# Mixing on four 32-row tiles of the array in place of a block-diagonal matrix

## The reference

```python
x: (32, 32, 256)   itok: (32,) in 1..198   weights: (200, 32, 32)
w_gate, w_up: (256, 1024)   w_down: (1024, 256)          # all float32

w = weights[itok]                                # a 32x32 matrix for each of 32 samples
y = einsum('bct,bcd->bdt', x, w)                 # the mixing
h = silu(y @ w_gate) * (y @ w_up)                # (32, 32, 1024)
h = of every 4 neighbours the 2 largest by magnitude, the others 0
out = x + h @ w_down
```

## Time and profile before

| | |
|---|---|
| median of three runs | 83.60 us |
| the profiled execution, its own time | 83.66 us |
| its span, first to last instruction | 81.7 us |
| PE busy | 75.5 us (92%) |
| DVE busy | 61.2 us (75%) |
| ACT busy | 42.9 us (53%) |
| mean granted TensorE clock | 0.994 |

### The profile page before, as it was taken

One profiled execution on the slowest core, in us unless ns is written; L12 is line 12 of the kernel. 1 busy time (PEld: TensorE's weight loads), 2 busy tenths in 40 slices (PEclk: granted clock), 3 DMA queues, 4 the chain that ended last, 5 costly groups with the idle time before them and its releaser, 6 DMA issues.

```text
span 81.7 us, 983 instructions
## 1 busy us (share of the span) xinstructions
PE 75.5 (92%) x338; PEld 59.8 (73%) x338; DVE 61.2 (75%) x93; ACT 42.9 (53%) x65; POOL 8.0 (10%) x13
## 2 busy tenths in 40 slices
PE   3996699999999999999999999999999999999920
PEld 1331688898888888888888888888888888888800
DVE  0003799178389999996899999999999999991060
ACT  6000983595863986975392699995770006410000
POOL 7500000000000070013000000442000000000000
PEclk9999999999999999999999999999999999999997
DMA  0792899977400049915800000399950000006024
GB/s 0 138 326 113 251 325 335 429 237 285 201 0 0 0 88 199 195 32 96 160 4 0 8 4 0 64 193 201 205 108 0 0 0 0 0 0 257 0 92 164
DMA packets 3076, 9.62 MB, mean 118 GB/s; under 512 B 480, under 2 KB 480, under 8 KB 2816
## 3 DMA queue, kind: packets, MB, share of 16 engines
q1 hardware_dynamic: 2160, 6.29, 22.3%
q0 software_dynamic: 912, 3.28, 20.9%
HBM read 5.37 MB, written 1.05 MB: 79 GB/s over the span
## 4 chain that ended last, share of the span: by engine, by line
PE 84%; DMA 8%; DVE 3%; ACT 1%; issue 1%; DVEq 0%
PE bank L536 50%; PE y_banks L573 13%; PE bank L573 13%; DMA h<-in_table,rows_sb 5%; PE y_banks L521 5%; PE bank L547 4%; DMA cond_sb<-in_cond 2%; DVE gate_raw L428 2%; ACT h L237 1%; DVE h L347 1%; DVE rows_sb L432 0%; DVEq L427 0%
## 5 line engine op out<-in xcount | busy, mean ns | idle before, releaser
L536 PE MATMUL bank<-y_hl,up_hl 128*128 128x512 f32 x96 | 24.2, 389 | 0.0
L536 PE MATMUL bank<-y_hl,gate_hl 128*128 128x512 f32 x84 | 21.4, 390 | 0.0
L536 PEld LDWEIGHTS bank<-y_hl,up_hl 128*128 128x128 f32 x96 | 18.0, 188 | 3.8
L536 PEld LDWEIGHTS bank<-y_hl,gate_hl 128*128 128x128 f32 x84 | 15.7, 188 | 3.2
L243 ACT ACTIVATE silu<-bank 128x512 f32<-128x512 f32 x16 | 9.4, 595 | 8.5 <-PE bank L536 8.2
L264 ACT ACTIVATE h_hl<-h 128x1024 fp32r<-128x1024 f32 (+1 forms) x8 | 6.7, 844 | 8.5 <-DVE h L414 8.4
L573 PE MATMUL y_banks<-h_hl,down_hl 128*128 128x512 f32 x48 | 11.0, 389 | 0.0
L573 PE MATMUL bank<-h_hl,down_hl 128*128 128x512 f32 x48 | 11.0, 389 | 0.0
L573 PEld LDWEIGHTS y_banks<-h_hl,down_hl 128*128 128x128 f32 x48 | 9.0, 188 | 1.9
L573 PEld LDWEIGHTS bank<-h_hl,down_hl 128*128 128x128 f32 x48 | 9.0, 188 | 1.9
L378 DVE TENSOR_TENSOR h<-bank,silu 128x512 f32<-128x512 f32 x12 | 8.1, 684 | 1.9 <-ACT silu L243 1.9
(11 more groups left out here) (40 smaller groups left out, 71.9 us busy)
## 6 DMA issues: line engine op xcount, KB each, us to landing
h_hl<-h POOLq DMA_DIRECT2D x4, 512.0 KB, 5.2
up_raw<-in_w_up SPq DMA_DIRECT2D x2, 512.0 KB, 5.8
down_raw<-in_w_down SPq DMA_DIRECT2D x1, 1024.0 KB, 9.5
gate_raw<-in_x_t SPq DMA_DIRECT2D x1, 1024.0 KB, 5.0
down_hl<-down_raw POOLq DMA_DIRECT2D x2, 512.0 KB, 5.5
out<-gate_raw SPq DMA_DIRECT2D x4, 256.0 KB, 2.3
x_sb<-in_x SPq DMA_DIRECT2D x2, 256.0 KB, 4.0
gate_raw<-in_w_gate SPq DMA_DIRECT2D x2, 256.0 KB, 4.4
```

Source lines behind the costliest of these rows:

```text
L536: last = nc.tensor.matmul(dst, w_hl[w][:, s, q, k, j], y_hl[:, m, half, k], start=i == 0, stop=i == len(terms) - 1)
```

## The change

The block-diagonal matrix is gone: POOL no longer zeroes it and ACT and DVE no longer copy blocks. Each 32x32 matrix is used where the transpose leaves it, by a matmul of 32 rows (one sample's channels), 128 stationary columns (a block k of x) and 32 moving columns. The four samples of a group use the array's rows 0 to 31, 32 to 63, 64 to 95 and 96 to 127, and write to four different PSUM banks. `mixing(half)` thus has 32 products where it had 8, and raises `mixed` once, at its end, where it raised it after each k. y of half 0 lies in banks 0 to 3, y of half 1 in banks 2 to 5; the pairs sit in banks 4-5, 6-7 and 0-1. `mixing(1)` is moved behind pair 2 and also waits for `product(0)`, since banks 4 and 5 held pair 0. The DVE's y_lo of half 0 waits for both pieces of y_hi, and `first_gates` takes the two y_lo terms last. Samples are dealt to halves and groups in another order on the host.

```diff
-        ring = [ctx.enter_context(nc.psum_tensor(f"bank{i}", [P, TH], f32)) for i in range(2 * RING)]
-        y_banks = ctx.enter_context(nc.psum_tensor("y_banks", [P, KT, TH], f32))
+        banks = ctx.enter_context(nc.psum_tensor("banks", [P, 8, TH], f32))
+        Y_BANK = 2
+        y_banks = banks[:, Y_BANK:Y_BANK + KT]
+        PLACES = [4, 6, 0]
+        MIX_BANKS = [0, Y_BANK]
+        MIX_PAIR = 3
+        def place(n):
+            return n % RING if n < MIX_PAIR else (n - MIX_PAIR + 1) % RING
+        def mixed_y(half, k, end):
+            y = banks[:, MIX_BANKS[half]:MIX_BANKS[half] + NB, 0:KT * P]
+            return y.rearrange("p r (k n) -> p k r n", k=KT)[:, k:end]
+        def split_y(part, half, k, end):
+            return y_hl[:, part, half, k:end].rearrange("p k (r n) -> p k r n", r=NB)
...
-            nc.gpsimd.memset(mix_diag, 0.0).then_inc(zero_done, 1)
...
             def high_y(half, k, end):
-                act.wait_ge(mixed, KT * half + end)
-                nc.scalar.activation(y_hl[:, HI, half, k:end], y_banks[:, k:end], ACT.Copy).then_inc(y_hi, 1)
+                act.wait_ge(mixed, half + 1)
+                nc.scalar.activation(split_y(HI, half, k, end), mixed_y(half, k, end), ACT.Copy).then_inc(y_hi, 1)
...
-            diagonal(ACT_FIRST)
...
-            diagonal(ACT_LAST)
...
             def low_y(i):
                 half, k, end = Y_PIECES[i]
-                dve.wait_ge(mixed, KT * half + end)
-                dve.wait_ge(y_hi, i + 1)
+                dve.wait_ge(y_hi, KT if half == 0 else i + 1)
...
-            diagonal(DVE_FIRST)
...
-            diagonal(DVE_LAST)
...
             def mixing(half):
+                pe.wait_ge(transposed, 1)
                 pe.wait_ge(x_in[half], 32 if half == 0 else 16)
                 if half > 0:
                     pe.wait_ge(y_lo, KT * half)
+                    pe.wait_ge(h_done, 1)
                 for k in range(KT):
                     for i in range(GH):
                         g = half * GH + i
...
-                        last = nc.tensor.matmul(y_banks[:, k, i * P:(i + 1) * P],
-                                                x_sb[:, g, k * P:(k + 1) * P],
-                                                mix_diag[:, g].rearrange("p b d -> p (b d)"),
-                                                start=True, stop=True)
-                    last.then_inc(mixed, 1)
+                        for r in range(NB):
+                            rows = slice(r * C, (r + 1) * C)
+                            last = nc.tensor.matmul(mixed_y(half, k, k + 1)[:, 0, r, i * D:(i + 1) * D],
+                                                    x_sb[rows, g, k * P:(k + 1) * P],
+                                                    mix_w[rows, g * D:(g + 1) * D],
+                                                    start=True, stop=True)
+                last.then_inc(mixed, 1)
...
-                terms = [(s, m, k) for k in range(KT) for s, m in ((HI, HI), (LO, HI), (HI, LO))]
+                terms = [(s, HI, k) for k in range(KT) for s in (HI, LO)] + [(HI, LO, k) for k in range(KT)]
...
             def gate_up(n):
-                if n >= RING:
-                    pe.wait_ge(h_done, n - RING + 1)
+                if n == MIX_PAIR + RING - 1:
+                    pe.wait_ge(y_lo, len(Y_PIECES))
+                elif n >= MIX_PAIR:
+                    pe.wait_ge(h_done, n - RING + (2 if n < MIX_PAIR + RING - 1 else 1))
...
-                if n == 2:
+                if n == MIX_PAIR:
                     mixing(1)
```

More of the change, by code:

```diff
@@ L74, in adaln_ffn @@
         mix_w = h[:, 1, 1, 0:NG * D]
-        mix_diag = h[:, 1, 2:4].rearrange("p m t -> p (m t)").rearrange(
-            "p (g b d) -> p g b d", g=NG, b=NB)
         far = sb("far", [P, 4, TH], bf16)
@@ L92, in adaln_ffn @@
         rows_done = sem("rows_done")
-        zero_done = sem("zero_done")
         transposed = sem("transposed")
-        diag_done = sem("diag_done")
-        diag_act_done = sem("diag_act_done")
         mixed = sem("mixed")
@@ L122, in adaln_ffn @@
         block = ctx.enter_context(nc.Block())
+        def place(n):
+            return n % RING if n < MIX_PAIR else (n - MIX_PAIR + 1) % RING
         def gate_bank(n):
-            return ring[2 * (n % RING)]
+            return banks[:, PLACES[place(n)]]
         def up_bank(n):
-            return ring[2 * (n % RING) + 1]
+            return banks[:, PLACES[place(n)] + 1]
+        def mixed_y(half, k, end):
[3 more added lines that the diff above has]
+            return y_hl[:, part, half, k:end].rearrange("p k (r n) -> p k r n", r=NB)
         def down_bank(half, k):
-            return y_banks[:, k] if half == 0 else (gate_bank(ACC_PAIR), up_bank(ACC_PAIR))[k][:]
+            return y_banks[:, k] if half == 0 else (gate_bank(ACC_PAIR), up_bank(ACC_PAIR))[k]
         Y_PIECES = [(0, k, k + 1) for k in range(KT)] + [(1, 0, KT)]
[L136 to L149, removed]
         PIECES = [(0, w, k, k + 1) for w in range(2) for k in range(KT)] + \
@@ L242, in gate_silu @@
                     act.wait_ge(h_done, n - 2)
-                nc.scalar.activation(silu[:, n % 3], gate_bank(n)[:], ACT.Silu).then_inc(silu_done, 1)
+                nc.scalar.activation(silu[:, n % 3], gate_bank(n), ACT.Silu).then_inc(silu_done, 1)
             def absolute(n):
@@ L348, in transpose_rows @@
                                     mix_row.rearrange("p (e c) -> p e c", e=D8)).then_inc(transposed, 1)
[L350 to L354, removed]
             def low_weights(i):
@@ L364, in low_y @@
                 half, k, end = Y_PIECES[i]
-                dve.wait_ge(mixed, KT * half + end)
-                dve.wait_ge(y_hi, i + 1)
-                nc.vector.tensor_tensor(y_hl[:, LO, half, k:end], y_banks[:, k:end],
-                                        y_hl[:, HI, half, k:end].bitcast(f32), ALU.subtract).then_inc(y_lo, 1)
+                dve.wait_ge(y_hi, KT if half == 0 else i + 1)
+                nc.vector.tensor_tensor(split_y(LO, half, k, end), mixed_y(half, k, end),
+                                        split_y(HI, half, k, end).bitcast(f32), ALU.subtract).then_inc(y_lo, 1)
             def product(n):
@@ L377, in product @@
                     dve.wait_ge(h_lo_sent[0][j // 2], 16)
-                nc.vector.tensor_tensor(hs[u][:, j], up_bank(n)[:], silu[:, n % 3],
+                nc.vector.tensor_tensor(hs[u][:, j], up_bank(n), silu[:, n % 3],
                                         ALU.mult).then_inc(h_done, 1)
@@ L507, in warm_up @@
                 for _ in range(times):
-                    nc.tensor.matmul(ring[0][:], warm[:, 0:P], warm[:], start=True, stop=True)
+                    nc.tensor.matmul(gate_bank(0), warm[:, 0:P], warm[:], start=True, stop=True)
             def mixing(half):
+                pe.wait_ge(transposed, 1)
                 pe.wait_ge(x_in[half], 32 if half == 0 else 16)
@@ L546, in first_gates @@
                     for n in (0, 1):
-                        nc.tensor.matmul(gate_bank(n)[:], w_hl[0][:, s, 0, k, n], y_hl[:, m, 0, k],
+                        nc.tensor.matmul(gate_bank(n), w_hl[0][:, s, 0, k, n], y_hl[:, m, 0, k],
                                          start=i == 0, stop=i == len(terms) - 1)
@@ L557, in gate_up @@
                         continue
-                    last = split_product(dst[:], w, q, half, j)
+                    last = split_product(dst, w, q, half, j)
                 last.then_inc(pair_done, 1)
@@ L612 @@
     NB = P // C
-    cond = _np.asarray(inputs["itok_B_1_198"]).reshape(B // NB, NB).T
+    NH = 2
+    cond = _np.asarray(inputs["itok_B_1_198"]).reshape(NH, NB, -1).transpose(1, 0, 2).reshape(NB, B // NB)
     cond = _np.broadcast_to(cond[:, :, None], (NB, B // NB, CHUNKS))
@@ L623 @@
     sent = {
-        "x": x.reshape(B // NB, NB, C, T).transpose(1, 2, 0, 3).reshape(P, B // NB, T),
+        "x": x.reshape(NH, NB, B // NB // NH, C, T).transpose(1, 3, 0, 2, 4).reshape(P, B // NB, T),
         "x_t": x.reshape(B * C, T // P, P).transpose(2, 1, 0),
```

## The result

The changed kernel takes 84.42 us (median of 22 runs, 83.98 to 85.91), the kernel before, beside it, 83.78 (22 runs, 83.40 to 84.56). In 8 of the 22 runs of the changed kernel, all between 85.54 and 85.91 us, the mean granted clock was 0.972 to 0.978; in the other 14, 83.98 to 85.01 us, it was 0.991 or more. So the changed kernel is slower by 0.64 us between the two medians, and by 0.5% (0.45 us) with the clock up, where +3.5 us was forecast. Rival A gave +0.6 and 84.2; the profiled execution took 84.17 with a span of 82.4.

What follows compares the result with a forecast made beforehand. PE's own stream, and what stands ahead of its first mixing matmul, was taken as the bound. 1.63 + 1.72 + 0.16 = +3.5 us gave 87.1 us; the range was 83.9 to 92.0, the forecast's own 85.3 to 88.4.

Steps and rivals of the forecast that it cites:

- Rival A: Both mixings: four loads at once, p = 0.027; second mixing waits for product(0); +0.6, 84.2 us; chance 0.23.
- Step 1: Kernel start: without the diagonal, mixing waits for the transpose alone; first matmul at 8.16 in place of 8.86, -0.70.
- Step 2: Both mixings: 64 load-matmul pairs a half on 32 rows, one product taking one load time, 0.107, for two pairs.
- p: Both mixings: how often a 32-row pair of load and matmul can start, taken as 0.0535 us.
- +1.63: First mixing: first gates start at 12.40 against 10.77, with the 0.70 gained at the start already in it.
- +1.72: Second mixing: 64 x 0.0535 = 3.42 us in place of 1.70.
- 0.16 for the passage: Second mixing: array may run empty passing from 128-row to 32-row matmuls and back; 0.16 taken between nothing and 0.33.
- Step 3: Between first mixing and first gates: the single signal leaves PE idle 0.7 us; first gates keep their 2.86.
- Step 4: Second mixing, behind pair 2: starts at 20.73 without waiting for product(0), ended at 19.50; then +1.72 and 0.16.
- B: Both mixings: row tiles don't run side by side at all, p = 0.107; +10.3, 93.9 us; chance 0.13.
- D: Both mixings: a 32-row load costs a quarter and four run at once, p = 0.007; -0.85, 82.8 us; chance 0.07.
- C: Around the mixings: granted clock falls to the 1.2 GHz level, 12 matmuls costing 2.4 us; 89.5 or 91.9; chance 0.10.

Runs made afterwards that it cites:

- runs_of_two: Changed kernel with two products (four pairs) in a row on the same 32 rows before the next rows; 85.95 us.
- hybrid_split: Changed kernel, but half 1 block-diagonal ahead of pair 2, and first mixing's k blocks in separate banks with own signals; 83.98 us, ratio 0.998.
- early_wide: Changed kernel with 128 moving columns in the first mixing and the last weight piece behind the first silu and product(0); 84.40 us, ratio 1.0044.
- rows_outer: Changed kernel with sample row outermost, eight products on the same 32 rows before the next rows; 101.53 us.
- early_product: Changed kernel with the last weight piece moved behind the first silu on ScalarE and behind product(0) on VectorE; 84.98 us, ratio 1.0032.
- filled: Changed kernel with two more warm-up matmuls before the first mixing and two dummy matmuls between it and first gates; 85.65 us.
- wide kernels: Changed kernel, hybrid_split and early_product, each with 128 moving columns in place of 32 in the first mixing; 84.49, 83.94 and 84.40 us.
- tiles_second: Changed kernel with the first mixing block-diagonal as before, only the second on row tiles behind pair 2; 84.34 us, ratio 1.0025.

## Why the prediction was wrong

**Step 1, the start:** right. 8.13 where 8.16 was given, the transpose having ended 0.03 earlier.

**Step 2, the price of a pair:** this is the step that failed: p = 0.0535, in the sentence that the first load of the next product can run beside the second load of this one "but, if loads keep their order, not ahead of it". Loads do not keep their order between row tiles: with the two pairs of each product back to back, four tiles still load together, and runs_of_two shows that a queue four pairs deep on the same rows changes nothing (2.05 us). p is 0.027 and not 0.0535. In the sum, the +1.63 for first gates came out as +0.16 (10.93 against 10.77) and the +1.72 with 0.16 for the passage as +0.22; the wait before the second mixing, put at nothing, is +0.31. The sum with p = 0.027 is rival A's, 84.2, against a profiled 84.17. That it comes so close is in part luck: A has first gates at 10.71, and they start at 10.93, but the second mixing waits for product(0) in both and starts where A has it, at 19.5. The second reason, that a pair needs two issues of 0.03, was a misreading of the earlier trace rows: 0.03 lay between a load and its matmul at the start of a stage, and four pairs in the changed kernel start within 0.02.

**Step 3, behind the first mixing:** right in kind. The single signal leaves PE idle for 0.81, where 0.7 was given: 0.14 lie between the end of y_hi and the first gate matmul, where 0.03 was given. The last matmul's record was to be shorter by 0.08 with 32 columns; it is 0.27, as with 128. Nothing waits inside first gates (2.82). hybrid_split bears it out from the other side.

**Step 4, the second mixing:** the wait for product(0) was seen, with its transfer, but was put aside because the forecast's mixing came too late to meet it. It is 0.31. In early_wide, where product(0) is early, 0.09 is left ahead of the mixing, the price of passing to 32-row matmuls. With 64 x 0.027 = 1.73 for the pairs, 0.2 of the 1.92 is the way back to 128-row ones. Together that is 0.3, near the upper end of the 0 to 0.33 that was given, where 0.16 was taken.

**Rivals.** A had 0.23 and came true. B is excluded by p = 0.027 itself, and D by rows_outer, where a 32-row load is no shorter than a 128-row one. C, given 0.10 and a price of 2.4 us, happens beside A in 8 of 22 runs at 1.5 us; the price was too high because it took all 12 matmuls as slow, and in early_product the pitch is back at 0.23 after eight. Of the two reasons given with C, the idle time behind the mixing plays no part (filled), and the few columns that the mixing works on do by the counts of the wide kernels, with the reservations named there. The idle time ahead of the mixing stays open.

**What stays open.** Why the same program keeps its clock in one run and not in the next, that is, what makes the warm-up fast early in some runs and whether that or the idle time behind it decides; whether a wide first mixing keeps the clock on the chips on which the narrow one lost it; the one fall in tiles_second, whose only narrow mixing is the second; and whether the 0.1 to 0.2 us of the early product is real in the medians.

## What to carry to other kernels

Splitting a 128-row product into four 32-row ones left the first mixing as long as it was (1.99 us), because the four tiles take turns closely: the load's columns set the pace, and four loads share it. The gain of leaving out a preparation step is then paid back by what the new layout imposes elsewhere, here one late signal for two blocks and a move behind a pair that waits for another engine. And small matmuls ahead of a dense stretch can cost its clock: look at the granted clock of many runs, not of one profile. Widening their moving side while the loads hide it cost 0.08 us here and is worth a try.

## What the runs showed of the hardware

- Loads of 128 f32 columns follow each other on one row tile every 0.108 to 0.112 us at a granted clock of 1.00 and every 0.213 at 0.50, and four tiles start theirs within 20 ns.
- A row tile starts loading ahead of the tile in turn: in rows_outer when its turn is four pairs off, in runs_of_two when it is 12 pairs off.
- With 32 moving columns in the first mixing, product by product over the four tiles, the clock fell in 27 of 74 runs; with 128 moving columns, on other chips, in 0 of 36. In the three other orders it fell in all 12 runs, in runs_of_two too, whose mixing is as short.
- The gather's DMA took 4.45 to 5.08 us from one profile to the next in kernels that have the same instructions ahead of it.
